# One scale operation and one reciprocal on 60 columns for the block scales of x and of the h behind it

## What is computed

```
Q, K, V = xpos(X Wq), xpos_down(X Wk), X Wv
p = softmax(Q K^T) * 0.9^|n-m|
x = layernorm(X + p V)
gate, up = q4(x) q4(Wg)^T, q4(x) q4(Wu)^T
h = silu(gate) * up
out = layernorm(x + q4(h) q4(Wd)^T)
```

## Time and profile before

| | |
|---|---|
| median of 3 runs | 980.66 us (979.34 to 980.86) |
| the profiled execution's own time | 980.01 us |
| its span in the trace | 978.1 us (1.9 us lie around it) |
| granted TensorE clock, mean over the span | 0.997 |
| PE busy | 960.3 us, 98% |
| DVE busy | 866.3 us, 89% |
| POOL busy | 786.9 us, 80% |
| ACT busy | 641.3 us, 66% |

### The profile page before, as it was taken

The page is one execution under the profiler, slowest core; times in us unless marked ns, Lnnn a source line. Parts: engine busy times, 40 slices in busy tenths (PEclk is TensorE's granted clock), DMA queues, the critical chain, the costliest instruction groups (busy, mean ns, idle before and its releaser), DMA issues.

```text
span 978.1 us, 20226 instructions
## 1 busy us (share of the span) xinstructions
PE 960.3 (98%) x6002; PEld 869.6 (89%) x6002; DVE 866.3 (89%) x1995; ACT 641.3 (66%) x1576; POOL 786.9 (80%) x854
## 2 busy tenths in 40 slices
PE   8999999999999999999999999999999999999996
PEld 7788998989998999998998899888999899899886
DVE  6979988988988988999898898888898898999985
ACT  3656666677666667666667666657666667777664
POOL 5988888798888889788788888879787888877664
PEclk9999999999999999999999999999999999999999
DMA  9124244342433424324343434433243342333300
GB/s 319 45 84 132 93 136 125 103 136 82 154 106 97 144 84 152 122 82 133 110 141 113 136 98 139 121 105 126 93 146 104 108 136 82 98 108 109 104 22 22
DMA packets 116109, 111.25 MB, mean 114 GB/s; under 512 B 12576, under 2 KB 93728, under 8 KB 114080
## 3 DMA queue, kind: packets, MB, share of 16 engines
q1 hardware_dynamic: 115312, 108.91, 34.7%
q10 hardware_dynamic: 688, 1.05, 0.3%
HBM read 69.53 MB, written 40.37 MB: 112 GB/s over the span
## 4 chain that ended last, share of the span: by engine, by line
PE 88%; DVE 6%; issue 2%; DMA 2%; POOL 1%; SPq 1%; ACT 0%; POOLq 0%; DVEq 0%; ACTq 0%
PE ps_g L634 12%; PE ps_g L635 11%; PE ps_g L636 11%; PE ps_oy L634 9%; PE ps_oy L636 9%; PE ps_oy L635 9%; PE ps_s L634 6%; PE ps_s L635 6%; PE ps_s L636 6%; PE ps_t L643 4%; PE ps_oy L643 1%; DMA parking<-turned 1%; PE ps_oy L822 1%; PE ps_oy L821 1%; PE ps_s L683 1%
## 5 line engine op out<-in xcount | busy, mean ns | idle before, releaser
L2478 POOL TENSOR_TENSOR h<-h,hsc 128x704 f32<-128x704 f32 x126 | 168.5, 1337 | 77.1 <-DVE h L1843 43.2
L2585 POOL TENSOR_TENSOR prob<-prob,decay_t 128x512 f32<-128x512 f32 x128 | 164.0, 1298 | 0.5 <-ACT prob L1282 0.5
L634 PE MATMUL ps_g<-wgu_h,xqt_h 128*128 128x480 f32 (+1 forms) x380 | 148.8, 392 | 2.8 <-DVE xqt_l L1898 1.2
L634 PE MATMUL ps_oy<-v_h,pt_h 128*128 128x256 f32 x512 | 149.0, 291 | 0.1
L635 PE MATMUL ps_oy<-v_l,pt_h 128*128 128x256 f32 x512 | 144.7, 283 | 0.0
L636 PE MATMUL ps_oy<-v_h,pt_l 128*128 128x256 f32 x512 | 144.7, 283 | 0.0
L636 PE MATMUL ps_g<-wgu_h,xqt_l 128*128 128x480 f32 (+1 forms) x380 | 142.6, 375 | 0.0
L635 PE MATMUL ps_g<-wgu_l,xqt_h 128*128 128x480 f32 (+1 forms) x380 | 142.3, 374 | 0.0
L1794 DVE SCALAR_TENSOR_TENSOR th<-th,ps_g 128x240 f32<-128x240 f32 x183 | 72.0, 397 | 49.4 <-ACT th L1212 47.9
L634 PE MATMUL ps_s<-k_h,q_h 128*128 128x512 f32 x256 | 102.8, 402 | 0.0
L635 PE MATMUL ps_s<-k_l,q_h 128*128 128x512 f32 x256 | 100.1, 391 | 0.0
(11 more groups left out here) (273 smaller groups left out, 3106.3 us busy)
## 6 DMA issues: line engine op xcount, KB each, us to landing
parking<-turned SPq DMA_DIRECT2D x122, 256.0 KB, 2.0
landing<-parking SPq DMA_DIRECT2D x488, 64.0 KB, 2.0
rope_t<-rope SPq DMA_DIRECT2D x15, 1024.0 KB, 5.9
xres<-x SPq DMA_DIRECT2D x64, 128.0 KB, 2.1
out<-yout SPq DMA_DIRECT2D x63, 128.0 KB, 2.0
xin<-x_t SPq DMA_DIRECT2D x14, 512.0 KB, 4.3
first_rope<-rope SPq DMA_DIRECT2D x2, 512.0 KB, 7.5
decay_t<-decay SPq DMA_DIRECT2D x1, 960.0 KB, 12.1
```

Of the source, the lines that this page charges most:

```text
L634: pe.matmul(dst, a_h, b_h, start=(start and i == 0), stop=False)
L2478: return tt(blocks(dst), blocks(src), sc[:, which, at:at + n].unsqueeze(2).to_broadcast([P, n, QB]), ALU.mult)
L2585: tt(prob[:, keys], prob[:, keys], decay_t[:, lo:lo + CW], ALU.mult).then_inc(decayed, 1)
```

## The change

`xsc` and `hsc` become two parts of one tensor `xhsc` of 60 columns. In the lists of steps 3 to 62, `x_scales`, `x_reciprocals`, `h_scales` and `h_reciprocals` are replaced by `scales(three)` and `scale_reciprocals(three)`, each one instruction on all 60 columns (in step 3, which has no h yet, on the 16 of x). Both stand directly behind `h_max(four)`, so `scales` now waits for the maxima of x and of h. POOL's `h_units` waits for the common reciprocal. The lists behind step 62 keep their separate calls, and so the h of tile 59 and later keep their own.

```diff
-        xsc = sb("xsc", [P, 3, D // QB])
-        hsc = sb("hsc", [P, 3, F // QB])
+        xhsc = sb("xhsc", [P, 3, (D + F) // QB])
+        xsc = xhsc[:, :, 0:D // QB]
+        hsc = xhsc[:, :, D // QB:]
...
+            def scales(i):
+                wait(dve, xmax_done, i + 1)
+                wait(dve, hmax_done, i)
+                if i > 0:
+                    block_scales(xhsc, xscale_done)
...
+            def scale_reciprocals(i):
+                wait(dve, xscale_done, i + 1)
+                if i > 0:
+                    reciprocals(xhsc, xinv_done)
...
                 if s // NT == NB - 1 and j > 0:
-                    x_scales(three)
                     h_max(four)
-                    x_reciprocals(three)
-                    h_scales(four)
+                    scales(three)
+                    scale_reciprocals(three)
                     turn(one, 0)
-                    h_reciprocals(four)
                     second_residual(five)
...
                 elif j == 2:
                     row_inverse(two)
-                    x_scales(three)
                     h_max(four)
-                    x_reciprocals(three)
-                    h_scales(four)
+                    scales(three)
+                    scale_reciprocals(three)
                     second_residual(five)
                     turn(one, 0)
-                    h_reciprocals(four)
                     landed_low(two)
...
                 elif j == 3:
-                    x_scales(three)
                     h_max(four)
-                    x_reciprocals(three)
-                    h_scales(four)
+                    scales(three)
+                    scale_reciprocals(three)
                     landed_low(two)
-                    h_reciprocals(four)
                     second_residual(five)
...
                 elif j == 4:
                     turn(one, 0)
-                    x_scales(three)
                     h_max(four)
-                    x_reciprocals(three)
+                    scales(three)
+                    scale_reciprocals(three)
                     turn(one, 1)
                     second_residual(five)
-                    h_scales(four)
                     landed_low(two)
                     x_shift(three)
-                    h_reciprocals(four)
...
                 elif j == 5:
-                    x_scales(three)
                     h_max(four)
-                    x_reciprocals(three)
-                    h_scales(four)
-                    h_reciprocals(four)
+                    scales(three)
+                    scale_reciprocals(three)
                     second_residual(five)
...
             def h_units(i):
-                    wait(pool, hinv_done, i + 1)
+                    if i < LAST_SCALED:
+                        wait(pool, xinv_done, i + 2)
+                    else:
+                        wait(pool, hinv_done, i - LAST_SCALED + 1)
```

More of the change, by code:

```diff
@@ L51 @@
 LAST_TILE = TILES - 1
+LAST_SCALED = LAST_TILE - 4
 R2_BEHIND = 3
@@ L421, in build @@
         w_units = "p (u n) -> p u n"
-        w_scale_buffers = (r2, yout, xv, hsc, r2)
+        w_scale_buffers = (r2, yout, xv, xhsc, r2)
         def w_values(m):
@@ L1821, in h_max @@
                     block_max(h[:, i % 2, 0:F], hsc, hmax_done)
+            def scales(i):
[3 more added lines that the diff above has]
+                    block_scales(xhsc, xscale_done)
+                elif i == 0:
+                    block_scales(xsc, xscale_done)
+            def scale_reciprocals(i):
+                wait(dve, xscale_done, i + 1)
+                if i > 0:
+                    reciprocals(xhsc, xinv_done)
+                elif i == 0:
+                    reciprocals(xsc, xinv_done)
             def h_scales(i):
@@ L1829, in h_reciprocals @@
                 if live(i):
-                    wait(dve, hscale_done, i + 1)
+                    wait(dve, hscale_done, i - LAST_SCALED + 1)
                     reciprocals(hsc, hinv_done)
```

## The result

The changed kernel takes 990.28 us (median of 4 runs, 989.54 to 991.08), beside 980.04 for the kernel before on the same chip: a ratio of 1.0106, with a 95% interval of 1.0092 to 1.0119. The forecast was 985.1 and +0.5%, within 980.0 to 988.0. The direction is right, the size is off by a factor of two, and the time lies above the range. The profiled execution took 989.54, with a span of 987.7.

The account below looks back on a forecast made before the run. PE was taken to bound the kernel, so late DVE results cost and saved DVE work doesn't. 3.85 + 1.0 + 0.35 - 0.45 = +4.75 us on a median of 980.66; forecast 985.1, range 980.0 to 988.0.

Parts of the forecast that it names:

- What bounds the kernel: Whole kernel: PE, busy for 98% of the span, sets the end; DVE work merely taken away buys nothing.
- The zero distances at `x1_transposes`: In `j` 5 and the last batch, x arrives 0.06 to 0.08 us before PE needs it, so no slack.
- The prices on DVE: From `h_max`'s start S: common scale 0.16 us, reciprocal 0.50; x's reciprocal at S + 1.63, 0.59 later than before.
- `j` 5: Seven steps: x's late reciprocal makes `gate_up` about 0.55 us late in each, 3.85 us in all.
- The last batch: Its `j` 1 to 6, six steps: later `second_residual` costs PE about 0.17 us each, 1.0 us in all.
- `j` 1 moves x by 0.03: Steps of `j` 1: PE's end of `down` holds `second_residual`, so x moves only 0.03 us, booked at nothing.
- In `j` 6, POOL comes out of other work later than the reciprocal: Steps of `j` 6: POOL's other work covers the later reciprocal, as in `j` 2; booked at nothing.
- The gain in `j` 3: Five steps waiting for `v_low`: 0.33 us gained is eaten by the late landing; 0.08 to 0.09 each remains, -0.45 us.
- rival C: `j` 2 and last batch: `turn(one, 0)` 0.3 to 0.5 later, 13 steps lose another 0.3: 989 us; chance 0.1.
- Rival A: All merged lists: fewer DVE instructions, x's lateness doesn't reach PE, so faster, 977 to 978.5 us; chance 0.1.
- the cover of `j` 4: In `j` 4, x's later chain costs nothing, as PE arrives some 0.8 us after x.

Follow-up runs that it names:

- the series: Kernel before, order_alone, scale_alone, one_wait and changed kernel, compared by x's reciprocal (0 to 0.76 us later) and mean `j` 5 step (0 to +0.74 us).
- one_wait: The changed kernel with one semaphore for both kinds of maxima, so that the common scale waits once: 986.23 us, 1.0053.
- undo_j5: The changed kernel with the old list of separate scales and reciprocals in `j` 5 alone: 983.8 us, 1.0036.
- order_alone: The changed kernel with four separate scale and reciprocal instructions behind `h_max` in place of the two common ones, in every list: 981.58 us, 1.0003.
- scale_alone: The changed kernel with one wait and the common scale, but two separate reciprocals, x's first: 985.16 us, 1.0038.
- before_turn_j2: The kernel before with `turn(one, 0)` of `j` 2 moved ahead of `h_max`: 976.79 us, 0.9961.
- turn_first_j2: The changed kernel with `turn(one, 0)` of `j` 2 moved ahead of `h_max`: 987.68 us, 1.0063.
- after_load_late: The changed kernel with the second parking of `j` 2 ahead of the load of x in SP's queue: 985.95 us, 1.0053.

## Why the prediction was off

**What bounds the kernel: right.** DVE work taken away was worth nothing. The zero distances at `x1_transposes` did mean zero slack, but they aren't what gives the series its slope of 1; the part that the prediction added behind them, by `h_units`, `h_magnitude` and `x1_high` to `gate_up`, is the path that decides, and it had that path right.

**"The prices on DVE": the step that failed.** It put x's reciprocal at S + 1.63; it came at S + 1.80. Of the 0.17, 0.08 is the second wait in `scales` (0.12 for 0.04; `one_wait` shows 0.03), 0.06 the scale on 60 columns, and 0.03 the reciprocal (0.528 for 0.50, inside my bounds). I had priced the scale by rows whose start overlaps the instruction before. The earlier trace rows give 0.16 on 44 columns; where the input has just come, the kernel before shows 0.20, in step 33, and the 60 columns take 0.216:

```profile
493.06 0.20 DVE L1785 TENSOR_SCALAR_CACHE_REDUCE hsc<-hsc 128x44 f32<-128x44 f32 x1
```

The 0.17 stands in every exposed step. `j` 5: 0.55 + 0.17 is 0.72, measured 0.74. The last batch: 0.17 + 0.17 is 0.34, measured 0.32. Together that is 2.2 us more than the sum had.

**"`j` 1 moves x by 0.03": wrong for the same reason.** With the reciprocal at S + 1.63, `x_units` would have started at S + 1.71 and let `x_magnitude` start at S + 2.36; S is 1.84 into step 33, so that is 4.20, against 4.12 before, 0.08 late. With 0.17 more it is 0.25, and six steps cost 1.49 us. A cover that was 0.1 wide was booked as a cover.

**"In `j` 6, POOL comes out of other work later than the reciprocal": right in all seven steps, and not enough.** `x_units` doesn't move by more than 0.05 in any of them. In four, the distance of 0.47 behind `h_max` makes DVE's own list late, and `x_shift` with it by 0.27 to 0.31. No row of before shows that distance, and its cause stays open.

**The gain in `j` 3: wrong in sign.** I set the 0.33 that `h_reciprocals` gives back against a landing 0.33 late, and took the rest as a gain. In step 34 `turn` was 0.42 late and the copy 0.57. In all six steps `turn` was 0.42 to 0.46 late, but the copy 0.27 to 1.52, and the step up to 1.15. The second parking takes 4.1 to 4.7 us in both kernels, so it isn't slower by the change; together with the landing behind it, it varies from step to step by as much as the loss, and what makes it vary isn't shown. With the parking ahead of the load, all six copies start 1.14 to 1.16 into the step, without a wait. This is rival C, at the place that it named in `j` 2; the part of it in the last batch did not come. How much it costs changes from one execution to the next: `j` 3 sums to +3.08, +0.05, +0.39 and +1.23 with the last batch in the changed kernel, `one_wait`, `undo_j5` and `order_alone`. The 2.77 of the table is one draw.

**Rival A's** condition was a `second_residual` earlier than S + 1.51; it is at S + 1.71. "Perfetto Trace Analysis", section "Optimizing Scalar/DVE Operations", in the Trainium skill, prefers splitting where an engine isn't saturated and holds others up; the series agrees, with 0.41 us a step between four instructions (`order_alone`) and two with one wait (`one_wait`). The other rule, to minimise the number of operations and not of semaphores ("VectorE: DVE Perf Modes", "Rules for kernel authors", in the Trainium skill), isn't borne out here: 177 instructions fewer gained no DVE time, and one semaphore wait fewer a step gave some 3 us of the loop. The same line of it advises against fusing chained operations for speed, and with that these runs agree.

**What it adds up to.** Of the 8.0 us by which the loop's sum was short, 2.2 are the mis-priced chain in `j` 5 and the last batch, 1.5 `j` 1, 1.1 `j` 6, 3.2 `j` 3 (this execution), and the rest is in `j` 2, 4 and 0 (0.1, 0.5 and -0.7). The last two are one step each. Step 4's 0.46 is the change's: it is 0.17, 0.31 and 0.40 in `order_alone`, `scale_alone` and `one_wait`, with `xqt_low` 0.18, 0.32 and 0.41 late, and 0 in the kernels without merging, so the cover of `j` 4 did not hold in its first step. Step 56's -0.69 isn't: it goes with POOL's product of the landed probabilities, which starts 10.88 us into the step before, 10.21 in the changed kernel, 11.31 in `order_alone` (+0.42) and 10.36 in `before_turn_j2` (-0.53), which merges nothing.

## What to carry to other kernels

When two chains meet at one instruction, the earlier one takes over the later one's lateness; before merging them, write down when each result is needed, by every queue that passes it on, and merge only where the early one has slack to spare. Price a dependent instruction by a row that starts behind its input, not by one that overlaps its predecessor, and count the waits ahead of it. A cover of 0.1 us is no cover when the price has an error of 0.2: `j` 1 was booked at nothing and cost 1.5 us.

## What the runs showed of the hardware

- A second semaphore wait ahead of a dependent DVE instruction cost 0.085 us: distances of 0.119 to 0.121 behind `h_max` with two waits, 0.034 to 0.035 with one.
- With two waits, the same pair in `j` 6 of every second batch stands 0.47 to 0.50 apart, in the changed kernel, `turn_first_j2` and `after_load_late` alike, and not in `one_wait`, `scale_alone` or `undo_j5`. `undo_j5` keeps both waits in `j` 6 and yet lacks it, so the second wait alone doesn't set it. What does isn't known; no run was made for it.
- Two short DVE instructions that don't depend on each other overlap by 0.08 to 0.09, and their rows then read short (0.16 for 0.20 on 44 columns).
- The 3.1 us outside the loop go with PE's granted clock. Near the end of the kernel before's profile (columns: window, its length, busy us of PE, PEld, DVE, ACT and POOL with instructions, granted clock, DMA share, GB/s):

```profile
960.00:964.00 4.00, 1.93 (x16) 1.62 (x15) 3.10 (x10) 2.06 (x6) 1.99 (x3) 1.00 0.01 2
964.00:968.00 4.00, 4.00 (x24) 4.00 (x24) 3.22 (x9) 1.67 (x6) 3.22 (x7) 0.62 0.02 8
```

and in the changed kernel at the same place of the program:

```profile
971.00:975.00 4.00, 1.93 (x16) 1.60 (x16) 3.07 (x11) 1.97 (x6) 2.08 (x3) 1.00 0.02 6
975.00:979.00 4.00, 4.00 (x34) 4.00 (x35) 3.32 (x9) 1.67 (x5) 3.12 (x7) 1.00 0.00 1
```

After the same half-idle 4 us, one execution goes on at a mean of 0.62, that is at the lower of the levels of 1.2 and 2.4 GHz for a part of the 4 us, and issues 24 matmuls; the other stays at 1.00 and issues 34. The 10 matmuls are 4.00 x 10 / 34 = 1.2 us of the 1.4 that differ there. At the start it is the same: from 20 to 25 us the kernel before has 0.71 and 24 matmuls, the changed one 1.00 and 37, and 1.7 us differ up to step 3. It comes and goes between executions, and isn't the change's: behind step 62, `before_turn_j2`, which merges nothing, takes 60.05 us at the full clock, and `after_load_late`, which merges in every list, takes 61.50 with such a stretch.
